# Softmax self-attention in a twelve-stage perceiver: the projected rows leave PSUM by ScalarE and reach x by GpSimd, and the bias becomes a product with ones

## The reference, cut to what matters

```python
qkv = x @ Wqkv.T + bqkv
q, k, v = jnp.split(qkv, 3, axis=-1)
q = q.reshape(b, s, N_HEADS, D_HEAD)          # k and v likewise
q = _rmsnorm(q, wq)                           # k likewise, with wk
attn = jnp.einsum('bqhd,bkhd->bhqk', qf, kf)
attn = jax.nn.softmax(attn, axis=-1)
z = jnp.einsum('bhqk,bkhd->bqhd', attn, vf).astype(x.dtype)
z = z.reshape(b, s, d)
return z @ Wo.T + bo
...
x = x + _L2_attn_ref(_layernorm(x, axis=-1), ...)
```

## Time and profile before

| | |
|---|---|
| time, median of 3 runs | 2775.71 us (2772.74 to 2777.46) |
| the profiled execution's own time | 2775.8 us |
| its span on the chip | 2774.0 us |
| TensorE busy in the span | 2512.8 us (91%) |
| VectorE busy | 1701.0 us (61%) |
| ScalarE busy | 1389.6 us (50%) |
| GpSimd busy | 732.0 us (26%) |
| the stage's first and last instruction | 2152.6 us, 2241.0 us |

### The profile page before, as it was taken

One profiled execution on the slowest core, in us unless ns is written; L12 is line 12 of the kernel. 1 busy time (PEld: TensorE's weight loads), 2 busy tenths in 40 slices (PEclk: granted clock), 3 DMA queues, 4 the chain that ended last, 5 costly groups with the idle time before them and its releaser, 6 DMA issues. The chain is left out here.

```text
span 2774.0 us, 84786 instructions
## 1 busy us (share of the span) xinstructions
PE 2512.8 (91%) x36489; PEld 2132.3 (77%) x36489; DVE 1701.0 (61%) x3422; ACT 1389.6 (50%) x3486; POOL 732.0 (26%) x1090
## 2 busy tenths in 40 slices
PE   7999888999968999999999867996998878999988
PEld 6888656777757899999997667995777756999577
DVE  6877675666657333333324664657887877777663
ACT  3888424555432444444442323435886544777342
POOL 3232102212102300000000303433445735666300
PEclk9999999999988999999999978997999999999999
DMA  3110003212021100000000032325220003111000
GB/s 98 37 37 21 1 0 99 63 33 63 3 63 61 48 17 17 17 17 17 2 2 25 3 131 92 126 81 183 89 89 1 3 2 100 54 50 48 1 1 31
DMA packets 118228, 126.76 MB, mean 46 GB/s; under 512 B 10877, under 2 KB 110152, under 8 KB 117864
## 3 DMA queue, kind: packets, MB, share of 16 engines
q1 hardware_dynamic: 114024, 110.93, 12.9%
q0 software_dynamic: 3840, 10.49, 1.2%
HBM read 105.67 MB, written 15.73 MB: 44 GB/s over the span
## 5 line engine op out<-in xcount | busy, mean ns | idle before, releaser
L1157 ACT ACTIVATE s_ca_probs<-s_ca_scores,s_ca_neg_max 128x256 f32<-128x256 f32 x768 | 352.7, 477 | 35.3 <-DVE s_ca_neg_max L1203 26.3
L1203 DVE TENSOR_REDUCE s_ca_neg_max<-s_ca_scores 128x4 f32<-128x1024 f32 x192 | 233.7, 1219 | 46.5 <-PE s_ca_scores L1056 25.3
L2212 DVE COPY s_mx_w_mixed<-s_mx_ps 128x512 f32<-128x512 f32 x256 | 163.6, 684 | 96.6 <-PE s_mx_ps L2058 83.1
L1073 PE MATMUL s_ca_probs_flipped<-identity,s_ca_probs 128*128 128x128 f32 x1536 | 210.6, 280 | 1.7 <-ACT s_ca_probs L1157 1.7
L1073 PEld LDWEIGHTS s_ca_probs_flipped<-identity,s_ca_probs 128*128 128x128 f32 x1536 | 164.4, 141 | 40.1 <-issue 20.8
L2167 ACT COPY s_mx_w_mixed<-s_mx_ps 128x512 f32<-128x512 f32 x256 | 137.3, 589 | 108.7 <-PE s_mx_ps L2045 86.1
L1157 ACT ACTIVATION_READ_ACCUMULATOR s_ca_probs<-s_ca_scores,s_ca_neg_max 128x1 f32 x768 | 160.3, 209 | 0.0
L1164 ACT COPY s_ca_probsT<-s_ca_probs_flipped 128x512 f32<-128x512 f32 x192 | 115.2, 600 | 77.7 <-PE s_ca_probs_flipped L1073 77.7
L300 POOL TENSOR_SCALAR x_normed_transposed<-x_normed_transposed,h_cc_rstd,h_cc_shift 128x256 f32<-128x256 f32 x56 | 30.6, 555 | 446.7 <-PE s_cc_out L1450 271.3
L971 POOL TENSOR_TENSOR s_ca_inv_spread<-s_ca_inv_sums,h_ca_own_half 128x128 f32<-128x128 f32 x192 | 72.6, 399 | 287.2 <-DVE s_ca_inv_sums L1225 287.2
L82 PE MATMUL s_cc_shared<-s_cc_ctxT_low,h_cc_wkv_high 128*128 128x256 f32 x512 | 146.0, 285 | 2.2 <-DVE s_cc_ctxT_low L1556 2.2
(11 more groups left out here) (571 smaller groups left out, 7554.4 us busy)
## 6 DMA issues: line engine op xcount, KB each, us to landing
h_ca_ctxT<-in_ctxT SPq DMA_DIRECT2D x96, 256.0 KB, 3.4
h_mx_w_by_input<-in_L_ffn_eW1T SPq DMA_DIRECT2D x16, 512.0 KB, 5.4
h_mx_w_by_hidden<-in_L_ffn_eW2T SPq DMA_DIRECT2D x8, 1024.0 KB
h_re_win<-in_L_ffn_W_in SPq DMA_DIRECT2D x8, 1024.0 KB, 5.9
h_ca_ctx<-in_ctx SPq DMA_DIRECT2D x32, 256.0 KB, 2.8
x_normed_transposed<-in_ctx SPq DMA_DIRECT2D x7, 1024.0 KB, 5.4
h_re_wout<-in_L_ffn_W_out SPq DMA_DIRECT2D x8, 512.0 KB, 3.8
choice_results<-s_rt_zeros SPq DMA_DIRECT2D x4, 1024.0 KB, 10.6
```

Source lines behind the costliest of these rows:

```text
L1073: last = nc.tensor.transpose(psT[u % len(psT)][:, 2 * a + c, :], PR[b % 2][:, 4 * n + 2 * h + a, c * P:(c + 1) * P], ident[:, :])
L1157: last = nc.scalar.activation(PR[b % 2][:, p, :], psS[:, p // 2, (p % 2) * NKEY:(p % 2 + 1) * NKEY], ACT.Exp, bias=nmax[b % 2][:, p:p + 1] ...
L1203: nc.vector.tensor_reduce(nmax[b % 2][:, 4 * n:4 * n + 4], psS[:, 2 * n:2 * n + 2, :].rearrange("p r (g k) -> p r g k", g=GR), AX_X, ALU.m ...
L2212: last = nc.vector.tensor_copy(part(int(name[1]), r), bank(j, r))
```

## The change

The projected rows no longer go from PSUM straight into x. ScalarE copies `psY` to one of two new tiles in SBUF, `YB`, and raises `s_yc`; GpSimd waits for that and adds `YB` to x; it then raises `s_x`, which lets VectorE take the statistics. VectorE's `update` is gone. GpSimd's `add_bias` is gone too: the bias enters `psY` as a product of one row of `ones` with one row of `BO`, which opens the sum that the two products by `WO` continue. TensorE waits for `s_yc` where it waited for `s_x`. `ones` is handed to the function.

```diff
-def softmax_attention(nc, X, ST, QKT, VA, ident, held):
+def softmax_attention(nc, X, ST, QKT, VA, ident, ones, held):
...
+        YB = [sb("sm_out", [P, DIM]) for _ in range(2)]
...
-                def add_bias(i):
-                    nc.gpsimd.tensor_tensor(X[:, i, :], X[:, i, :], held.BO[:, :], ALU.add).then_inc(s_xb, 1)
+                def add(i):
+                    pool.wait_ge(s_yc, i + 1)
+                    nc.gpsimd.tensor_tensor(X[:, i, :], X[:, i, :], YB[i % 2][:, :], ALU.add).then_inc(s_x, 1)
...
-                pool.wait_ge(s_w, 48)
                 for i in range(TILES):
-                    add_bias(i)
                     normalise(i)
                     if i + 2 < TILES:
                         spread(i + 2)
+                    if i:
+                        add(i - 1)
+                add(TILES - 1)
...
                     if i:
                         pe.wait_ge(s_at, i)
-                        pe.wait_ge(s_x, i)
+                        pe.wait_ge(s_yc, i)
...
                 def output(i):
                     pe.wait_ge(s_at, i + 1)
-                    if i:
-                        pe.wait_ge(s_x, i)
+                    nc.tensor.matmul(psY, ones[0:1, :], held.BO[0:1, :], start=True, stop=False)
                     for c in range(KC):
-                        last = nc.tensor.matmul(psY, AT[i % 2][:, c, :], WO[:, c, :], start=(c == 0), stop=(c == KC - 1))
+                        last = nc.tensor.matmul(psY, AT[i % 2][:, c, :], WO[:, c, :], start=False, stop=(c == KC - 1))
                     last.then_inc(s_y, 1)
...
+                def out(i):
+                    act.wait_ge(s_y, i + 1)
+                    if i >= 2:
+                        act.wait_ge(s_x, i - 1)
+                    nc.scalar.copy(YB[i % 2][:, :], psY).then_inc(s_yc, 1)
+
                 exponentiate(0)
                 for i in range(TILES):
                     if i + 1 < TILES:
                         exponentiate(i + 1)
+                    if i:
+                        out(i - 1)
                     turned(i)
                     attended(i)
+                out(TILES - 1)
...
-                def update(i):
-                    dve.wait_ge(s_y, i + 1)
-                    dve.wait_ge(s_xb, i + 1)
-                    nc.vector.tensor_tensor(X[:, i, :], psY, X[:, i, :], ALU.add).then_inc(s_x, 1)
...
-                    if 1 <= i <= TILES:
-                        update(i - 1)
```

More of the change, by code:

```diff
@@ L2875, in softmax_attention @@
         psY = psO[0][:, DIM:2 * DIM]
-        s_par, s_q, s_s, s_xb = sem("parity_ready"), sem("queries_spread"), sem("scores_ready"), sem("x_biased")
+        s_par, s_q, s_s, s_yc = sem("parity_ready"), sem("queries_spread"), sem("scores_ready"), sem("out_copied")
         s_mx, s_mv, s_e, s_sum, s_ri, s_p = (sem("max_ready"), sem("scores_moved"), sem("exponentials_ready"), sem("sums_ready"),
@@ L3848, in perceiver @@
                     normed_heads(nc, X, XNT, QKT, VA, ident, h, norm)
-                    softmax_attention(nc, X, ST, QKT, VA, ident, a)
+                    softmax_attention(nc, X, ST, QKT, VA, ident, ones, a)
             layernorm_transposed(nc, X, XNT, ident, ST, by_position=True)
```

## The result

The changed kernel takes 2787.7 us (median of 12 runs) against 2778.3 us for the kernel before (12 runs, among them the three that the prediction started from, whose median was 2775.71). The ratio is 1.0033, 95% interval 1.0023 to 1.0043: slower by 9.2 us, between 6.4 and 11.9. One of the twelve runs of the changed kernel was slow, 4883.7 us; the ratio leaves it out, and the median of the other eleven is 2787.0. The forecast was slower by 7.5 us (a ratio of 1.0027), at 2783.2 us, with a range up to 2786.5. The sign and what sets the pace were right, the growth lies inside the measured interval, and the time lies outside the range, 1.2 us above its upper end.

The account below looks back on a forecast made before the run. A 4.61 us loop through VectorE and ScalarE bounds a tile; the one-row product's 0.63 us lifts TensorE's 4.36 to 4.99, which takes over. The stage grows by 7.5 us: 2775.71 + 7.5 = 2783.2 us, range 2778.5 to 2786.5.

Parts of the forecast that it names:

- what sets the pace: In the stage's steady tiles TensorE, at 4.99 us a tile, takes over from the VectorE and ScalarE loop's 4.61.
- The update is worth nothing to VectorE in steady tiles: Removing VectorE's update, 16 x 0.41 us, gains nothing in steady tiles, since the wait that it filled stays.
- GpSimd's and ScalarE's new steps cost nothing in steady tiles: GpSimd's add costed at nothing, at most 0.73 us a tile; ScalarE's copy at nothing, at most 0.37 us a tile.
- The one-row product costs 0.63 us: On TensorE per tile, ahead of the output product: 0.32 us first record, 0.31 second record and switch to 128 rows.
- split of the 7.5 us: Stage growth: 4.9 us in 13 steady tiles, 0.6 in tile 0, the rest in the two last tiles.
- Rival A: The switch of rows on TensorE is hidden: product 0.43 us, stage grows by 4.3 us, 2780.0 us; chance 0.16.
- Markers: Flips 4.95 to 5.05 us apart, one-row product 0.6 ahead, VectorE idle about 0.4 before the maximum, no probability wait.
- the next one starts behind it as before, and nothing in it changes: The stage after the changed one only starts later, behind a growth of 7.5 us, and is otherwise unchanged.
- 4.36 + 0.63 for all 13 tiles: TensorE's tile becomes 4.99 us, thirteen times over, from flips of tile 1 at 2172.16 to tile 14 at 2237.03.
- Some 2 us: The forecast's own spread, from 0.05 us a tile and from earlier runs between 2772.74 and 2777.46 us.
- cases of the tile's pace alone: The range's cases, from a hidden switch (2780.0 us, chance 0.16) to ScalarE's copies delaying attend (2785 to 2788, 0.07).

Follow-up runs that it names:

- e2: The changed kernel without the product of ones, the bias left out of the output; 2779.5 us, ratio 1.0008.
- e7: e2 with VectorE summing the exponentials in two halves, the first while ScalarE still makes the second; one execution, 2778.9 us.
- e1: The changed kernel with identity times 128 equal bias rows in place of the one-row bias product; 2779.9 us, ratio 1.0013.
- after: The changed kernel itself; median 2787.7 us, ratio 1.0033, its profiled execution 2784.1 us.
- p1: The changed kernel with 20 in place of 12 identity products ahead of the first tile's flips; one execution, 2790.3 us.
- e3: The kernel before with the one-row bias product in place of GpSimd's bias add, VectorE's update kept; 2788.9 us, ratio 1.0045.
- e6: The changed kernel with two unread identity products in TensorE's wait ahead of the one-row product; 2786.5 us, ratio 1.0028.
- e8: The changed kernel with the bias product in 128 full rows and two more identity products ahead of it, behind the wait; 2786.8 us, ratio 1.0033.
- a1: The changed kernel measured once more, no edit; 2786.4 us, ratio 1.0044.
- p2: The kernel before with 20 in place of 12 identity products ahead of the first tile's flips; one execution, 2776.0 us.

## Why the prediction was right, and where it failed

- **The update is worth nothing to VectorE in steady tiles.** Right: e2 keeps 4.61 us a tile and shows the wait of 0.36 us bare.
- **GpSimd's and ScalarE's new steps cost nothing in steady tiles.** Right at this pace: e2 against before, 59.7 and 59.6 us for 13 tiles; 0.7 us at the end, forecast 0.8. e7 shows that the cover is thin: at 4.40 us a tile ScalarE's copy delays attend by 0.28 us in every second tile.
- **The one-row product costs 0.63 us, 0.32 for its first record and 0.31 with the switch.** Right: 1.59 - 0.96 = 0.63 us, and the tile 4.36 + 0.63 = 4.99. Its split of the 7.5 us is a little off, its sum is not: tile 1 took 4.37 us before and not 4.61, so the 13 tiles were to grow by 5.3 us and not 4.9. e1 gives the split: 0.44 us for the product, 0.19 for the change of rows. Rival A, the switch hidden, is refuted, and e1 measured its price: 4.80 us a tile, ratio 1.0013, which is 3.6 us for the rival's 4.3.
- **Markers.** Flips 4.99 us apart (forecast 4.95 to 5.05), the one-row product 0.62 us ahead of the output product (0.6), no wait for probabilities. VectorE's idle time ahead of the maximum is 0.24 us and not 0.4: the rest of its slack, 0.36, lies ahead of the sum.
- **The step that failed** is "the next one starts behind it as before, and nothing in it changes", and, in the sum, 4.36 + 0.63 for all 13 tiles: both take the granted clock as it was before. The sum had no term for it. Measured in place of nothing: 1.6 to 3.3 us in the tiles in each of the four executions; 0.7 to 0.8 us in the last tile in three of them (after, p1 and e3: 1.89 to 1.95 us for its product by WO in place of 1.13); and in nine of the ten kernels with any part of the change, 1.1 to 2.3 us in the next stage (13.7 to 15.0 us against 12.6 in the three without). The first of these is tied to the one-row product by e1, e6 and e8, but for the pace of 4.99 us. For the third the runs name no single part: e2, without the product, has it as well as e3, without copy and add, and e8 has it not. With copy and add at the end, TensorE stands idle for 1.97 us ahead of the next stage's first products and not for 1.23, as the rows above show; that this lets the clock fall is not shown, since e8 has the same 1.97 us and e3 has 1.23.
- **The range failed by its start as well.** 2775.71 was the median of three runs; twelve give 2778.3. Of the 4.5 us between forecast and measurement 2.6 are this, and 1.9 the growth, 9.4 (2787.7 - 2778.3) for 7.5. The profiles give more: from the stage to the end of the span, without the chance at the stage's start, after and a1 take 12.5 and 12.2 us more than before, p1 10.6 more than p2. Why the medians give less the runs don't show. "Some 2 us" of spread was too little: twelve runs of before lie between 2772.7 and 2781.3, and the unchanged stages ahead of this one vary by 8 us between executions. And the range was built from cases of the tile's pace alone, so its upper end had no room for a clock that falls.

## What to carry to other kernels

Work that fills a wait inside a loop of several engines can be free, as the update was here; to move it to another engine then gains nothing, and what is put behind the wait on the engine that is next in line can set the new pace. A bias as a one-row product is not a small thing ahead of full products: here the switch of rows cost nearly as much again (0.19 us) as one of its two records (0.22); the identity with a bias that lies in all rows does the same sum for less. When an edit puts thin work next to a wait on TensorE, allow for the clock in the range, and look at the granted clock of the stretch, and of the stages behind it, before comparing spans.

## What the runs showed of the hardware

- A product of one row ahead of products of 128 rows cost 0.19 us more than one of 128 rows with the same columns (4.99 against 4.80 us a tile). The loads took the same time, 0.182 and 0.188 us; the load engine stood idle for 0.33 us at the switch, and not at all without it.
- With the one-row product behind a wait of 0.52 us, TensorE's granted clock averaged 0.74 to 0.81 over stretches of 9 to 16 us inside the tiles in four of four executions, all at 4.99 us a tile; with the wait filled, or with full rows, even in a tile of 5.24 us, it stayed at 1.00 there. The same eight flips took 1.04 us at the upper level and 1.91 at the lower one.
- Extra products of the identity that nothing reads, put into the wait (e6), cost 0.05 us a tile, and the clock stayed at 1.00: the 13 tiles were 1.0 to 2.7 us shorter than without them. The whole time, 2786.5 us, was not better.
- Stages that no edit touches took 532.8 to 533.2 us behind this one in the three kernels without any part of the change, and 533.8 to 539.1 in the ten with some of it.
